# A selective scan inside a four-layer network: the scan begun in the stage before it, its step inputs in spare columns of a decay's bank

## The reference

```
xz = einsum('bhwc,ec->bhwe', x, in_proj_w); xin, z = split(xz, 2)
xc = silu(depthwise_conv3x3(xin) + conv_b)
xs = stack([x0, x1, x0[..., ::-1], x1[..., ::-1]])        # rows, columns, both reversed
x_dbl = einsum('bkdl,kcd->bkcl', xs, x_proj_w)            # 8 step + 16 B + 16 C rows
dt = softplus(einsum('bkrl,kdr->bkdl', dts_r, dt_proj_w) + dt_proj_b)
h = h * exp(dt_l * A) + (dt_l * u_l) * B_l                # for every token l
y = einsum('bkdn,bkn->bkd', h, C_l)
...
y = layer_norm(y + Ds * xs) * norm_g + norm_b
return einsum('bhwd,cd->bhwc', y * silu(z), out_proj_w)
```

## Time and profile before

| | us |
|---|---|
| median of 3 runs | 11165.92 |
| the profiled execution's own time | 11187.02 |
| its span | 11185.2 |
| POOL, drive of a state (L669), x1536 | 2756.4 |
| DVE, scan (L653), x1536 in two groups | 1801.3 and 871.2 |
| PE, identity matmuls (L557), x6144 | 2373.1 |
| ACT, decay (L582), x1536 | 1370.6 |
| DVE, weighing (L640), x768 | 1126.8 |

### The profile page before, as it was taken

The page is one execution under the profiler, slowest core; times in us unless marked ns, Lnnn a source line. Parts: engine busy times, 40 slices in busy tenths (PEclk is TensorE's granted clock), DMA queues, the critical chain, the costliest instruction groups (busy, mean ns, idle before and its releaser), DMA issues. The chain is left out here.

```text
span 11185.2 us, 139472 instructions
## 1 busy us (share of the span) xinstructions
PE 8980.1 (80%) x42716; PEld 6002.8 (54%) x42716; DVE 7179.1 (64%) x9364; ACT 4559.6 (41%) x8465; POOL 4134.1 (37%) x2895
## 2 busy tenths in 40 slices
PE   4777777777776777699999999589568989897567
PEld 2434343334433434599999999578323333333455
DVE  6999799979988998445444444211356666552446
ACT  4666566656665665222222222123214444444221
POOL 4999599859986997111111111000000000000001
PEclk8898888988988889899999999667769999998678
DMA  3444344434444443100000000310310000002110
GB/s 122 156 159 156 104 155 158 144 115 155 159 131 130 156 158 121 33 13 11 13 13 9 13 13 7 85 36 6 123 48 17 13 17 13 17 13 95 38 28 17
DMA packets 335205, 831.25 MB, mean 74 GB/s; under 512 B 37778, under 2 KB 111894, under 8 KB 324060
## 3 DMA queue, kind: packets, MB, share of 16 engines
q1 hardware_dynamic: 334628, 823.93, 23.4%
...
## 5 line engine op out<-in xcount | busy, mean ns | idle before, releaser
L669 POOL TENSOR_TENSOR ss_work<-ss_dtu,ss_ringb 128x768 f32<-128x768 f32 x1536 | 2756.4, 1818 | 3.8
L557 PE MATMUL ss_ps<-ss_work,ss_ident 128*128 128x512 f32 (+1 forms) x6144 | 2373.1, 538 | 263.1 <-DVE ss_work L640 156.8
L557 PEld LDWEIGHTS ss_ps<-ss_work,ss_ident 128*128 128x128 f32 x6144 | 1249.4, 210 | 1165.4 <-issue 762.6
L653 DVE TENSOR_TENSOR_SCAN ss_work<-ss_ps,ss_last,ss_work 128x768 f32<-128x768 f32 x1024 | 1801.3, 1798 | 0.0
L582 ACT ACTIVATE ss_ps<-ss_dt,ss_a_neg 128x768 f32<-128x768 f32 x1536 | 1370.6, 892 | 173.9 <-DVE ss_work L653 166.9
L640 DVE TENSOR_TENSOR ss_work<-ss_work,ss_ps 128x1280 f32<-128x1280 f32 x768 | 1126.8, 1467 | 137.4 <-ACT ss_ps L582 118.1
L1169 ACT ACTIVATE stu_XT<-cv_ps 128x384 fp32r<-128x384 f32 x768 | 377.7, 492 | 1779.1 <-DVE cv_ps L1216 1331.2
L2204 DVE TENSOR_REDUCE at_top<-at_ps 128x384 f32 (+1 forms) x1728 | 888.7, 552 | 259.3 <-PE at_ps L2123 259.2
L2186 ACT ACTIVATE at_probs<-at_ps 128x768 f32<-128x768 f32 x864 | 696.3, 811 | 867.7 <-PE at_ps L2140 867.6
L653 DVE TENSOR_TENSOR_SCAN ss_work<-ss_ps,ss_work 128x768 f32<-128x768 f32 x512 | 871.2, 1738 | 64.2 <-POOL ss_work L669 64.2
L1605 POOL MEMSET c_pooled<- 128x2048 f32 x2 | 3.6, 1808 | 2292.5 <-POOLq L59 2292.5
(11 more groups left out here) (538 smaller groups left out, 15558.2 us busy)
## 6 DMA issues: line engine op xcount, KB each, us to landing
ss_ringb<-scan_rows SPq DMA_DIRECT2D x768, 384.0 KB, 3.7
ss_ringc<-scan_rows SPq DMA_DIRECT2D x768, 384.0 KB, 3.8
...
at_packs<-at_parts SPq DMA_DIRECT2D x192, 144.0 KB, 3.2
...
```

The source lines that it names most:

```text
L557: ins = pe.matmul(acc[:, d * WIN + a:d * WIN + e], ident[:, :], weighed[:, t % DEEP, d, a:e], start=False, stop=n == NST - 1, skip_group_c ...
L653: dve.tensor_tensor_scan(hid[:, t % DEEP, d, ::step], decay[d][:, ::step], drive[:, t % DEEP, d, ::step], start, ALU.mult, ALU.add).then_i ...
L669: pool.tensor_tensor(drive[:, t % DEEP, d, :], dtu[:, t // NST % 2, d, :], ringb[:, t % RING, :], ALU.mult).then_inc(s["driven"], 1)
```

## The change

- `XT` of the next image is loaded during the scan (at t = 8), the first one in the setup block. The DRAM copy of the transposed input gets 2304 more columns, so that the last image has something to load.
- The twelve gate projections and their SiLU move from the third block into the first, four behind each of PE's convolved chunks; `sz` gets memory of its own. `ON_PE` falls from 4 to 3.
- Step inputs, exp and log of section 0 are made in the first block, between the last products; adding the parts and multiplying with the input is DVE's there. The even rows go to DRAM a chunk at a time, the odd ones at the block's end, and the first two B rows and the first C row are loaded before the block ends. DVE's and POOL's first weighings wait for the stores, since they overwrite `rowsb`.
- For sections 1 to 11 a state has at most one "job" on PE, written to `side`, the 256 columns behind the first decay in its second bank: a step input in states 0, 1, 2, 3, 5, 6, and in 8 to 13 the sum relu(z) + log(...) as two identity matmuls. Because bank and decay are shared, the job of state t waits on PE until the decay (t, 0) is written, and DVE's scan (t, 0) waits until ACT has copied the job's result. ACT makes |z|, exp, log and ReLU over 768 columns at a time. POOL no longer adds.
- `acc` is kept a half at a time, at n = 1 and n = 2; a bank used by one half alone is started by the first matmul's flag, and only the bank of both is zeroed. `y`'s window is added at n = 3 to 6.

```diff
-    ON_PE = 4
+    ON_PE = 3
+    GATES = D2 * NCH
+    AHEAD = 2
...
+                if c == AHEAD:
+                    pe.wait_ge(s["even_kept"], AHEAD)
+                if c >= AHEAD and c < AHEAD + D2:
+                    step_input(2 * (c - AHEAD))
+                    step_input(2 * (c - AHEAD) + 1)
...
+                if c >= NCH - D2 - 1 and c < NCH - 1:
+                    d = c - (NCH - D2 - 1)
+                    dve.wait_ge(scan["soft"], d + 1)
+                    dve.scalar_tensor_tensor(dt[:, 0, d, :], dt[:, 0, d, :], 0.0, dtu[:, 0, d, :], ALU.max, ALU.add).then_inc(scan["added"], 1)
+                    dve.wait_ge(scan["added"], d + 1)
+                    dve.tensor_tensor(dtu[:, 0, d, :], dt[:, 0, d, :], xc[:, d, 0:WIN], ALU.mult).then_inc(scan["dt_ready"], 1)
...
-    FIRST_Y, KEEP_AT = 10, 2
+    SIDE = 256
+    side = flat[:, 1536 + WIN:1536 + WIN + SIDE]
+    INPUT_AT, SUM_AT = (0, 1, 2, 3, 5, 6), (8, 9, 10, 11, 12, 13)
+    SIZE_AT, EXP_AT, LOG_AT, RELU_AT, READY_AT = (3, 6), (4, 7), (5, 8), (7, 9), (10, 13)
+    FIRST_Y, KEEP_AT = 3, (1, 2)
...
+                if t == 2 * RING:
+                    sp.dma_start(XT[:, :], xt_dram[:, bass.ds(b * S + S, S)]).then_inc(pre["loaded"], 16)
...
+            def step_sum(i, d, at):
+                pe.wait_ge(s["bounded"], D2 * (i - 1) + d + 1)
+                pe.wait_ge(s["soft"], D2 * i + d + 1)
+                pe.matmul(side, ident[:, :], dt[:, i % 2, d, at:at + SIDE], start=True, stop=False, skip_group_check=True)
+                return pe.matmul(side, ident[:, :], dtu[:, i % 2, d, at:at + SIDE], start=False, stop=True, skip_group_check=True)
+
+            def beside(t):
+                if job(t):
+                    i, stage, d, at, _ = job(t)
+                    pe.wait_ge(s["decayed"], 2 * t + 1)
+                    (step_input, step_sum)[stage](i, d, at).then_inc(s["z_full"], 1)
...
+                if n == 0:
+                    if i:
+                        pe.wait_ge(s["kept"], D2 * (i - 1) + 1)
+                    add_weighed(t, 0, 0, 512)
+                    if i:
+                        beside(t + 3)
+                        pe.wait_ge(s["kept"], D2 * i)
+                    pe.matmul(ps[:, 1, :], zero[:, :], bc(zero[:, None, :], [P, 4, P]), start=True, stop=False, skip_group_check=True)
...
+                    if d == 0 and job(t):
+                        dve.wait_ge(s["z_kept"], job(t)[4])
```

More of the change, by code:

```diff
@@ L355, in _ @@
         def _(sp):
-            sp.dma_start(XT[:, :], xt_dram[:, bass.ds(b * S, S)]).then_inc(s["loaded"], 16)
-            sp.wait_ge(s["loaded"], 16)
+            for c in range(NCH):
+                sp.wait_ge(s["even_kept"], c + 1)
+                sp.dma_start(rows[0:64, at(c)], rowsb[0:64, at(c)]).then_inc(scan["first_stored" if c < AHEAD else "even_stored"], 16)
+                if c == AHEAD:
+                    sp.wait_ge(scan["first_stored"], 16 * AHEAD)
+                    for t in range(2):
+                        sp.dma_start(ringb[:, t, :], bass.AP(rows.tensor, t * S, [[0, P], [1, WIN]])).then_inc(scan[f"b{t}"], 16)
+                    sp.dma_start(ringc[:, 0, :], bass.AP(rows.tensor, 32 * S, [[0, P], [1, WIN]])).then_inc(scan["c0"], 16)
+            sp.wait_ge(s["odd_kept"], NCH)
+            sp.dma_start(rows[64:128, :], rowsb[64:128, :]).then_inc(scan["odd_stored"], 16)
         @block.gpsimd
@@ L408, in _ @@
                 act.activation(xc[:, 1, at(c)], ps[:, 6 + c % 2, 0:R], ACT.Silu, bias=convb[:, 1:2]).then_inc(s["gated"], 1)
+                if c < ON_PE - 1:
+                    for n in range(4 * c, 4 * c + 4):
+                        gate(n)
             act.wait_ge(s["conv_done"], 1)
@@ L411, in _ @@
                 act.activation(xc[:, 0, at(c)], y[:, 0, at(c)], ACT.Silu, bias=convb[:, 0:1]).then_inc(s["gated"], 1)
+            for n in range(4 * (ON_PE - 1), GATES):
+                gate(n)
             act.wait_ge(s["conv_done"], 2)
@@ L534, in _ @@
-            for t in range(3):
-                if step_chunk(t):
-                    pe.wait_ge(s["z_kept"], step_base(1) + step_chunk(t)[1])
-                    step_input(*step_chunk(t), 7)
+                    return pe.matmul(side, weights, dtr[:, n * WIN + at:n * WIN + at + SIDE], start=True, stop=True)
+                across = dtr[:, :].rearrange("p (h w) -> p w h", w=W)
+                for a, e in runs(n * WIN + at, n * WIN + at + SIDE):
+                    whole = a % 48 == 0 and e % 48 == 0
+                    source = across[:, a // 48:e // 48, :] if whole else across[:, a // 48, a % 48:a % 48 + e - a]
+                    ins = pe.matmul(side[:, a - n * WIN - at:e - n * WIN - at], weights, source, start=True, stop=True)
@@ L538, in _, with add_weighed @@
+            def add_weighed(t, d, a, e):
+                n = t % NST
+                return pe.matmul(acc[:, d * WIN + a:d * WIN + e], ident[:, :], weighed[:, t % DEEP, d, a:e], start=n == 0 and e - a == 512, stop=n == NST - 1, skip_group_check=True)
+            beside(0)
+            beside(1)
             for t in range(STATES):
                 i, n = t // NST, t % NST
-                if step_chunk(t + 3):
-                    pe.wait_ge(s["weighted"], t + 2)
-                    step_input(*step_chunk(t + 3), 7)
@@ L543, in _ @@
-                if n == 0:
-                    if i:
-                        pe.wait_ge(s["kept"], D2 * i)
-                    for bank in range(3):
-                        pe.matmul(ps[:, bank, :], zero[:, 0:P], zero[:, :], start=True, stop=False, skip_group_check=True)
+                if n != 1 or i == 0:
+                    beside(t + 2)
                 if 0 <= n - FIRST_Y < 2 * D2:
@@ L553, in _ @@
                 pe.wait_ge(s["pool_weighted"], t + 1)
[L554 to L558 removed]
+                if n == 0:
[6 more added lines that the diff above has]
+                    pe.matmul(ps[:, 1, :], zero[:, :], bc(zero[:, None, :], [P, 4, P]), start=True, stop=False, skip_group_check=True)
+                else:
+                    add_weighed(t, 0, 0, 512)
@@ L560, in _, with keep_step @@
+                add_weighed(t, 0, 512, WIN).then_inc(s["summed"], 1)
+                add_weighed(t, 1, 0, 256)
+                add_weighed(t, 1, 256, WIN).then_inc(s["summed"], 1)
         @block.scalar
         def _(act):
-            def keep_step(i, m, bank):
-                act.wait_ge(s["z_full"], step_base(i) + m + 1)
-                d, at, width = step_cut(i, m)
-                act.activation(dt[:, i % 2, d, at:at + width], ps[:, bank, 0:width], ACT.Relu)
-                act.activation(dtu[:, i % 2, d, at:at + width], ps[:, bank, 0:width], ACT.Abs).then_inc(s["z_kept"], 1)
+            def keep_step(t):
+                i, _, d, at, count = job(t)
+                act.wait_ge(s["z_full"], count)
+                act.activation(dt[:, i % 2, d, at:at + SIDE], side, ACT.Copy).then_inc(s["z_kept"], 1)
@@ L613, in _ @@
                 decays(t, 0)
[L614 to L615 removed]
+                if job(t):
+                    keep_step(t)
                 if t:
@@ L628, in _ @@
             copy_c(LAST)
-            keep_sums(len(SECTIONS) - 1)
+            for d in range(D2):
+                keep_sums(len(SECTIONS) - 1, d)
         @block.vector
@@ L747, in _ @@
             mean(1)
-            for n in range(D2 * NCH):
-                gate(n)
             for c in range(NCH + 2):
```

211 lines of the change are left out of this document (116 added, 95 removed).

## The result

The changed kernel takes 11224.84 us (11208.48 to 11227.34, five runs) against 11165.92; the ratio is 1.0049, 95% interval [1.0034, 1.0063]. It is half a per cent slower, where 1.3% faster was forecast. The profiled execution took 11227.34 us (span 11225.6), 40.4 us of span more than before.

The account below looks back on a forecast made before the run. DVE was taken to set the scan's pace, with stalls of 41.5 us an image above its floor. Savings of 25.8 - 3 + 37.6 + 13.6 + 72 = 146 us took the median from 11166 to 11020, range 10960 to 11100.

Parts of the forecast that it names:

- load of XT, less the larger store: PE's start in each image: waits for the load go, 25.8 us, less 3 for the larger transposed-input store.
- gates out of the block behind the scan: Block behind the scan: DVE's third centring no longer waits behind twelve gates, 9.4 us an image, 37.6 in all.
- block ahead of the scan and the scan's head: PE's start to first weighing: block 7.4 us longer, head 21.0 cut to 10.2; net 3.4 an image, 13.6.
- inside the scan: Scan sections: stalls of 41.5 us an image fall to 23, saving 18 an image, 72 in all; bounds 0 to 124.
- the rest of the program: Everything outside the changed stages: taken as untouched, with no term in the sum.
- The odd rows' store: Block's end: the first weighing waits for this store, expected in by then; forecast wrong if it holds the weighing.
- in time by 0.7: Scan: a 256-column job, copy and hand-overs take 1.3 us of the 2.04 available before the waiting scan.
- third rival: Scan: nearly all stalls go, 31 us an image, 124 in all; kernel at 10968 us; chance 20%.
- DVE's idle time ahead of the scan: Sign in the scan: names ACT's copy of `side`, about 20 us an image; over 60 would make the second rival true.
- the scan isn't shorter than 950: Sign that the forecast is wrong; an image's scan was expected to last about 940 us.
- second rival: Scan: jobs late for whole stretches, 2 to 2.9 us a state; kernel slower, 11230 to 11326 us; chance 8%.
- first rival: Scan: PE's lower clock eats the gain, sections still lose 4 us; 74 us saved, kernel at 11092; chance 17%.

Follow-up runs that it names:

- e11: e1 with column-direction step inputs read in row order (other tokens' values), so each job is one matmul: 11073.85 us, scan 945.1.
- e4: e1 with ACT's ReLU of the first half moved from n = 7 to n = 3: 11070.05 us, scan 944.9.
- e3: e1 with the rows of y's window added at n = 5, 11, 12, 13 instead of 3 to 6: 11084.16 us, scan 948.7.
- e10: e1 with ReLU at n = 3, y one piece per iteration from n = 6, section 0's state-3 job before the rest of state 0's sum: 11026.54 us.
- e1: Changed kernel with 60 more do-nothing increments on PE ahead of the spectral convolution's loop: 11152.72 us, ratio to before 0.9982.
- e8: Changed kernel with the original kernel's scan jobs in sections 1 to 11, keeping the 60 extra instructions: 11114.50 us, ratio to before 0.9950.

## Why the prediction was wrong

In the order of its sum, each term against the two traces:

| term | forecast | measured |
|---|---|---|
| load of XT, less the larger store | -22.8 | -26.4 |
| gates out of the block behind the scan | -37.6 | -38.7 |
| block ahead of the scan and the scan's head | -13.6 | +3.0 |
| inside the scan | -72 | +34.8 |
| the rest of the program | 0 | +76.0, and -8.3 that is not told from scatter |

The marks between the terms are, for each of the four images, PE's first projection, the first and the last weighing, and the end of the last addition. The right column adds up to the 40.4 us.

*Load of XT*: right. From the end of the last addition to PE's next first projection there are 8.65 us where there were 16.69 (first image to second); the mean of the three images is 7.6 us less, and the first projection of all comes 3.6 earlier. *Gates*: right, the third centring is 9.7 us earlier. *Block ahead*: the sign was wrong. The first weighing is 74.0 us behind the first projection in the second image, where I had forecast 69 and before it is 72.2 (1204.82 to 1277.00). Most of it is a term that the sum left out. The forecast works out 3.3 us for DVE's larger share of the convolution, and then adds up only 3.8 + 2.6 + 1 = 7.4. In the mean of the images the third copy of the rows comes 3.4 us later behind the first projection, the wait for the fourth product adds 3.8, and DVE's wait for the first logarithm (3.31 us), its add and its product add 3.2: 10.4, where all of its own terms would have given 10.7. The head shrank from 21.2 to 11.6, I had 10.2. The odd rows' store holds nothing, as forecast.

*Inside the scan* is the first step that failed. I wrote that a job of 256 columns takes 0.8 us and is "in time by 0.7", and had 2.1 us of waits a section in all. Three things were mis-sized or left out. The job of a column direction isn't one matmul but two or three pieces, as the kernel's `runs` cuts it: 1.27 us, and e11 puts 20.6 us an image on it, more than the 18 that I had forecast as the gain. ACT's two passes at n = 7 I had priced at 1.2 us a section, and e4 shows 20.8 us an image, 1.9 a section. And I had left y out of PE's queue over n = 3 to 6, where a sum of 2.8, y's 1.45 to 2.0 and a job of 1.27 make more than a state's 4.7; that is e3's 17 us. The parts overlap, so they don't add. At the boundary the old stall shrank at n = 1 (18.9 to 7.8), but 6.2 us came up at n = 2, 2.4 of them in section 0, so that n = 0 to 2 went from 20.8 to 17.5 only. e10, at 934.3 against 956.2 before, reaches 22 of the 31 us that the third rival gave the scan. Of the signs that I had named, DVE's idle time ahead of the scan is 48 us an image, between the 20 of the forecast and the 60 of the second rival, and the scan isn't shorter than 950.

The first rival comes nearest for this part (no gain in the scan, where 34.8 us were lost), but its reason is not what happened: PE's clock rose, from 0.89 to 0.91. The second rival's mechanism, scans that stand for late jobs, is what happened, only with 0.2 to 1.4 us at a time (2.3 once, in section 0), in up to seven states of a section, and not in whole stretches.

*The rest of the program* is the second step that failed: I put it at nothing. That "the rest of it isn't touched" is true of the code and not of its place. Against the forecast this step is 76 us and the scan 107, but it alone turns the change from slightly faster to slower. With it alone put right (e1) the change would be 0.2% faster, with the scan's jobs undone as well (e8) 0.5%. Shown: the stage's loss comes and goes with the loop's distance to a block's end (six kernels), in both programs, and it divides into 29.9 us of stops and about 44.4 us for the half rate. Not shown is what the loop of the mixer itself loses at its edge, and what makes the rest of the delay at n = 2.
